# Attention in a two-layer model: TensorE's loop over pairs of heads rolled up, with one buffer each for the pair's operands

## The chip, the cores and the metric

One core of a Trainium2 chip (trn2) runs the whole kernel. The metric is the device time in microseconds (us) of one execution. Engines: PE is TensorE (PEld its weight loads), DVE is VectorE, ACT is ScalarE, POOL is GpSimd, SP is SyncE, which here only issues DMAs.

## The reference

The kernel computes two layers on 4 sequences of 1024 tokens with 256 channels, in float32. The change touches only the attention of the second layer:

```python
q = xn @ Wq;  k, v = split(xn @ Wkv)            # 16 heads of 64
q = apply_rope(pos, q);  k = apply_rope(pos, k);  q = q * SCALE
sim = einsum('bhid,bhjd->bhij', q, k)            # causal mask
attn = softmax(where(causal_mask, neg, sim))
out = einsum('bhij,bhjd->bhid', attn, v)         # then out @ Wo
```

After it comes a mixture of 8 experts with 2 chosen per token, and `x + s * silu(ffn)`. Whoever follows the change needs nothing more of them.

## The kernel before

The program runs in stages: the first layer (`normalize`, `first_layer`, `experts`), then `attention(nc, d, "at", 0, 3, True)` for the first three sequences (the first part below), then `moe`, the experts of the second layer, and then `attention(nc, d, "at2", 3, 1, False)` for the fourth sequence together with the closing sum of the whole output (the second part).

Attention goes over *pairs* of heads, 8 pairs for each sequence: 24 in the first part, 8 in the second. What each engine does in a pair is written as a list of events (`PE_ORDER`, `ACT_ORDER`, `DVE_ORDER`, lines 1192 to 1198). An event with a plus sign belongs to the pair after this one. TensorE's list is

```python
PE_ORDER = ("A0+ A1+ S4.1 S5.0 S5.1 S6.0 S6.1 S7.0 S7.1 A2+ T4.0 A4+ A5+ T5.0 T6.0 T6.1 A6+ T7.0 T7.1 S0.0+ S1.0+ S2.0+ S3.0+ V0 V1 S4.0+ "
            "W0 W1 W2 W3")
```

- **A** (lines 1593, 1599): projections of the next pair. A0 and A1 make queries and keys of the first half of the tokens, A4 and A5 of the second, A2 and A6 the values. ScalarE copies queries and keys to `raw` (line 1700) and the values to `v_top` (first half, keys 0 to 511) and `v` (line 1694).
- SP swaps the halves of each head by DMA (`swap`, line 1408), and GpSimd rotates: `rotate(of, half)`, lines 1720 to 1731, three operations for each half of the tokens, `raw * cos`, `swapped * sin` and their sum, into `qkT`.
- **S** (line 1608): scores from `qkT`. VectorE takes the running maximum (line 1901) and ScalarE the exponential (line 1675).
- **T** (line 1614): turns the late keys' probabilities, which ScalarE copies to `pT` (line 1686). VectorE transposes the others in blocks (line 1919).
- **V0** (line 1629): values of the first 512 keys in 32-row blocks, from `v_blocks`, which SP fills from `v_top` with 16 DMAs (`replicate`, line 1415). **V1** (line 1641): values of the other keys, from `v`. ScalarE copies the result (line 1706).
- **W** (line 1650): output projection with `wo`. VectorE adds it to the output (line 1938).

One event's results lie in PSUM banks used in turn; before an event PE waits until the bank's last reader is done (`free`, line 1546), and on what the event needs. Written out, one pair holds some 60 such waits on PE.

Two copies of `w` (projection weights), `wo`, `qkT` and `v` exist, used by even and odd pairs (`x = (u + ahead) % 2`). On ScalarE and SP the pairs are a hardware loop (`Fori`) whose body is two pairs (`run`, line 1356). On PE, VectorE and GpSimd Python writes all pairs out one after another; PE's lines are 1655 to 1658:

```python
                pairs = nb * PAIRS
                act_on("first", -1, -1, 1, -1)
                for it in range(pairs):
                    act_on("both" if it < pairs - 1 else "last", it, it % PAIRS, it % 2, it // PAIRS)
```

In SP's order `pair(it, ...)` (line 1418) issues the next output weights, the swaps of pair `it + 1`, the projection weights of pair `it + 3`, what the stage adds (`ready`) and the replication. Weights of pairs 0 and 1 and the first output weights are loaded during the first layer (`d.at_loads`, line 2190). In the first part GpSimd also sends token rows to experts with 8 indirect DMAs after each of 8 pairs' rotations (lines 1765 to 1785), and copies out a sequence (`end`). In the second part it closes the output between rotations: `begin` sums two gathered rows, ScalarE takes a tanh ahead of `T7.1` (line 1668), `plus` and `finish` do the rest.

Of the kernel before, what the change touches and what calls it, by code (L numbers as in the profile page):

```python
# [14 lines left out]
ds = bass.ds  # L15

P = 128
# [31 lines left out]
class Steps:  # L49
# [17 lines left out]
    def wait(self):  # L67
# [19 lines left out]
           "y_out w_in0 w_in1 wo_in0 wo_in1 a_ps qk_read v_read swap_in0 swap_in1 cosed sined rot_done blocks_in turned blocks_read s_ps exp_done inv_done s_seen s_read t_ps "  # L87
# [4 lines left out]
    "at2": ("steps less_max expd masks counted counts_read routed known h_in0 h_in1 h_ready0 h_ready1 y_out w_in0 w_in1 wo_in0 wo_in1 a_ps "  # L92
# [1182 lines left out]
def attention(nc, d, name, b0, nb, scatter):  # L1275

    with ExitStack() as ctx:
# [3 lines left out]
        qkT = [d.moe_ya[:, TB * C + u * 2 * T:TB * C + (u + 1) * 2 * T] for u in range(2)]  # L1281
        v_top, v = d.moe_w1[:, 0:HALF * P], [s.sb(f"v{u}", HALF * P) for u in range(2)]
# [45 lines left out]
        w_in, wo_in = s.sems("w_in"), s.sems("wo_in")  # L1328
# [50 lines left out]
        with nc.Block() as block:  # L1379
            @block.sync  # L1380
            def _(sp):
                if scatter:
                    sp.dma_start(number[:, :], d.number).then_inc(numbered, 16)
                for u in range(2):
                    sp.sem_inc(w_in[u], 16)
                    if u == 0:
                        sp.sem_inc(wo_in[u], 16)
                    sp.sem_inc(h_in[u], 16 * KC)
                    sp.sem_inc(h_ready[u], PAIRS)  # L1389
# [20 lines left out]
                def replicate(of):  # L1410

                    sp.wait_ge(blocks_read, of * HALF + ONE)
                    for b in range(QB):
                        for a in range(QB):
                            sp.dma_start(v_blocks[a * QR:(a + 1) * QR, b * HALF * P:(b + 1) * HALF * P],
                                         v_top[b * QR:(b + 1) * QR, :]).then_inc(blocks_in, 16)

                def pair(it, u, load_w, load_wo, half_free=lambda half: None, ready=lambda: None):

                    sp.wait_ge(w_ps, it * 4 + ONE)  # L1420
                    sp.dma_start(wo[1 - u][:, :], load_wo).then_inc(wo_in[1 - u], 16)
# [4 lines left out]
                    if load_w is not None:  # L1426
                        sp.dma_start(w[1 - u][:, :], load_w).then_inc(w_in[1 - u], 16)
# [3 lines left out]
                def next_w(i, u):  # L1431
                    return d.w["qkv"][ds(i * (2 * P) + (3 + u) * P, P), :], d.w["wo1"][:, ds(i * (2 * C) + (1 + u) * C, C)]
# [8 lines left out]
                sp.dma_start(w[0][:, :], d.w["qkv"][2 * P:3 * P, :]).then_inc(w_in[0], 16)  # L1441
                if nb > 1:
                    with sp.Fori(0, nb - 1) as b:
                        with sp.Fori(0, PAIRS // 2 - 2) as i:
                            for u in range(2):
                                pair(b * PAIRS + (i * 2 + u), u, *next_w(i, u))
                        pair(b * PAIRS + (PAIRS - 4), 0, d.w["qkv"][(PAIRS - 1) * P:PAIRS * P, :], wo_of(PAIRS - 3))
# [856 lines left out]
```

## Time and profile before

| | |
|---|---|
| three timed runs | 2503.62, 2504.72, 2507.83 us (median 2504.72) |
| the profiled execution | 2504.4 us, its span 2502.6 us |
| granted TensorE clock, mean | 0.962 of 2.4 GHz |
| busy: PE, PEld, DVE, ACT, POOL | 2293.1, 1644.2, 1391.0, 932.5, 899.5 us |
| attention, first part | from 801 to 1761 us |
| experts of the second layer | 1762 to 2161 us |
| attention, second part | 2168 us to the end |
| q8 instruction queue | 141 packets, 2.31 MB |
| q14 instruction queue | 74 packets, 0.61 MB |

Times in rows count from the start of the span. A timeline row is: start, length, engine, line, operation, names of output and inputs, shape, how many instructions were merged, and in brackets how long the engine had been idle and what ended that; "issue" means that the profile shows nothing it waited for.
### The profile page before, as it was taken

To read this page: it belongs to the slowest core of one execution; us is meant where nothing else is said; L and a number is where in the kernel's file an instruction comes from. 1 tells how busy PE (TensorE), PEld (TensorE's weight loads), DVE (VectorE), ACT (ScalarE), POOL (GpSimd) and SP (SyncE) were. 2 spreads that over 40 slices of the span, in tenths; PEclk is the share of its full clock that TensorE was granted. 3 is DMA by queue.
4 is the path that set the end of the run, shared out by engine and by line. 5 is a ranking of instruction groups with operands and counts; after the bars stand their busy time and mean duration, and the time that the engine had idled before them with its cause. 6 is when DMAs were issued, how large, how long until landed. Compare 5 with 4: busy or idle time off the path is not lost. (4 is left out here: it accounts for less than half of the span.)

```text
span 2502.6 us, 57008 instructions
## 1 busy us (share of the span) xinstructions
PE 2293.1 (92%) x20696; PEld 1644.2 (66%) x20697; DVE 1391.0 (56%) x3950; ACT 932.5 (37%) x2197; POOL 899.5 (36%) x659
## 2 busy tenths in 40 slices
PE   7999999999987688788899999998899999799995
PEld 5555556655565456556577666776899999666664
DVE  6675332222236856566677787776333333377685
ACT  3211111111125335344455655554222222264562
POOL 3002001554446445545534443442111111256761
PEclk9999999999998889999999999998999999999998
DMA  6013103975447233433332333333676776355441
GB/s 216 17 51 118 48 19 110 277 213 163 118 107 239 71 100 101 128 89 109 103 81 73 93 102 88 99 82 113 242 245 235 239 242 235 98 145 161 146 113 59
DMA packets 158631, 330.84 MB, mean 132 GB/s; under 512 B 25056, under 2 KB 95216, under 8 KB 148048
## 3 DMA queue, kind: packets, MB, share of 16 engines
q1 hardware_dynamic: 137472, 284.98, 36.7%
q0 software_dynamic: 20944, 42.94, 6.6%
q8 instruction: 141, 2.31, 0.4%
q14 instruction: 74, 0.61, 0.1%
HBM read 193.61 MB, written 67.12 MB: 104 GB/s over the span
## 5 line engine op out<-in xcount | busy, mean ns | idle before, releaser
L1675 ACT ACTIVATE at_p<-at_p,at_nmax 128x640 f32<-128x640 f32 (+7 forms) x512 | 393.2, 771 | 214.9 <-DVE at_nmax L1901 214.6
L1901 DVE CUSTOM_DVE_ANT_0 at_p<-at_ps,atk_mask 128x512 f32<-128x512 f32 (+3 forms) x512 | 281.1, 581 | 190.2 <-PE at_ps L1608 142.4
L1919 DVE STREAM_TRANSPOSE at_pB<-at_p 128x512 f32<-128x512 f32 (+3 forms) x512 | 279.4, 586 | 122.4 <-PE at_ps L1629 109.6
L1608 PE MATMUL at_ps<-kept_big 64*128 64x512 f32 (+3 forms) x1536 | 289.9, 510 | 36.9 <-POOL kept_big L1731 12.2
L1725 POOL TENSOR_TENSOR kept_big<-kept_xg,atk_cos 128x1024 f32<-128x1024 f32 x64 | 151.4, 2366 | 403.7 <-ACT kept_xg L1700 403.7
L1593 PE MATMUL at_ps<-atk_h,atk_w 128*128 128x512 f32 x512 | 241.0, 615 | 12.5 <-SPq L1389 12.5
L1629 PE MATMUL at_ps<-at_pB,at_v_blocks 32*64 32x256 f32 (+1 forms) x8192 | 209.2, 344 | 22.3 <-issue 15.9
L1608 PEld LDWEIGHTS at_ps<-kept_big 64*128 64x128 f32 x1536 | 133.5, 190 | 141.0 <-issue 45.1
L1629 PEld LDWEIGHTS at_ps<-at_pB,at_v_blocks 32*64 32x64 f32 x8192 | 183.6, 133 | 59.0 <-DVE at_nmax L1901 27.1
L1938 DVE SCALAR_TENSOR_TENSOR kept_big<-at_ps,at_inv,kept_big 128x256 f32<-128x256 f32 x512 | 203.7, 475 | 31.7 <-PE at_ps L1650 31.6
L1065 PE MATMUL ex_ps<-kept_big 128*128 128x512 f32 x480 | 210.2, 596 | 0.9 <-ACT kept_big L1122 0.9
L2020 POOL DMA_INDIRECT z_rows<-late_yo,late_to x71 | 68.8, 969 | 379.8 <-DVE late_yo L2103 379.8
L2042 PEld LDWEIGHTS moe_ps<-moe_xT,moe_w 128*128 128x128 f32 x1696 | 197.6, 192 | 3.9 <-ACT moe_xT L2075 1.2
L2042 PE MATMUL moe_ps<-moe_xT,moe_w 128*128 128x128 f32 x1696 | 198.0, 275 | 1.0 <-ACT moe_xT L2075 1.0
L1728 POOL TENSOR_TENSOR kept_xg<-kept_xg,atk_sin 128x1024 f32<-128x1024 f32 x60 | 142.1, 2368 | 132.3 <-DMA kept_xg<-kept_xg 132.3
L1593 PEld LDWEIGHTS at_ps<-atk_h,atk_w 128*128 128x128 f32 x512 | 95.1, 196 | 120.9 <-issue 90.8
L1065 PEld LDWEIGHTS ex_ps<-kept_big 128*128 128x128 f32 x480 | 91.7, 191 | 110.6 <-issue 109.9
L1700 ACT ACTIVATE kept_xg<-at_ps 128x512 f32<-128x512 f32 x128 | 76.6, 598 | 234.7 <-PE at_ps L1593 232.1
L1731 POOL TENSOR_TENSOR kept_big<-kept_big,kept_xg 128x1024 f32<-128x1024 f32 x64 | 151.4, 2365 | 21.3 <-DVE kept_xg L1923 12.4
L1650 PE MATMUL at_ps<-atk_wo,at_oT 64*128 64x256 f32 x1024 | 126.8, 400 | 32.4 <-ACT at_oT L1706 32.4
L1650 PEld LDWEIGHTS at_ps<-atk_wo,at_oT 64*128 64x128 f32 x1024 | 107.2, 202 | 61.9 <-ACT at_oT L1706 43.3
L1151 DVE TENSOR_TENSOR kept_big<-kept_big,ex_ps 128x512 f32<-128x512 f32 x64 | 44.0, 687 | 186.5 <-ACT kept_big L1127 175.5
(249 smaller groups left out, 3651.4 us busy)
## 6 DMA issues: line engine op xcount, KB each, us to landing
moe_w<-in_w_w SPq DMA_DIRECT2D x53, 1028.0 KB
kept_xg<-kept_xg SPq DMA_DIRECT2D x256, 128.0 KB, 2.3
at_v_blocks<-atk_first_w SPq DMA_DIRECT2D x512, 64.0 KB, 2.0
atk_first_w<-in_w_w SPq DMA_DIRECT2D x18, 1028.0 KB, 4.4
atk_w<-in_w_qkv SPq DMA_DIRECT2D x32, 384.0 KB, 3.2
slot_in<-kept_big SPq DMA_DIRECT2D x9, 1032.0 KB
kept_big<-in_w_eg SPq DMA_DIRECT2D x16, 512.0 KB
kept_big<-in_w_eu SPq DMA_DIRECT2D x16, 512.0 KB
```

Of the source, the lines that this page charges most:

```text
L1065: last = pe.matmul(bank, w[:, k * F0 + f * P:k * F0 + (f + 1) * P], xT[u][k][:, :], start=k == 0, stop=k == KC - 1)
L1593: last = pe.matmul(banks[0], w[x][:, k * QKV + m * P:k * QKV + (m + 1) * P], h[:, k * T + half * CH:k * T + (half + 1) * CH], start=k == 0 ...
L1608: pe.matmul(banks[e][:, 0:to - at], qkT[x][e * DH:(e + 1) * DH, n * P:(n + 1) * P], qkT[x][e * DH:(e + 1) * DH, T + at:T + to], start=True ...
L1629: last = pe.matmul(banks[a][e * DH:(e + 1) * DH, k * QR:TB * QR], v_blocks[rows, at:at + DH], keys[:, b], start=k == 0 and b == 0, stop=False)
L1650: last = pe.matmul(banks[e][:, t * C:(t + 1) * C], oT[rows, (2 * n + t) * P:(2 * n + t + 1) * P], wo[u][rows, :], start=True, stop=True)
L1675: act.activation(buf, buf, ACT.Exp, bias=nmax[:, unit:unit + 1], scale=-1.0, accum_out=rsum[:, unit:unit + 1]).then_inc(exp_done, 1)
L1725: pool.tensor_tensor(out=out, in0=plain, in1=cos_of, op=ALU.mult).then_inc(cosed, 1)
L1731: pool.tensor_tensor(out=out, in0=out, in1=other, op=ALU.add).then_inc(rot_done, 1)
L1901: ins = dve.tensor_tensor_reduce(out=p[unit % LAG][:, at:to], in0=ring[BANK_OF["S", (t, c), e]][:, 0:to - at], in1=mask[:, 0:CH] if to <= ...
L1919: dve.transpose(strided(pB[e][:, t * P:(t + 1) * P], TURN_STEP, keys), tiles(p[unit % LAG][:, 0:keys * P], keys)).then_inc(turned, 1)
L1938: dve.scalar_tensor_tensor(out=part_y, in0=bank[:, t * C:(t + 1) * C], scalar=inv[:, unit:unit + 1], in1=part_y, op0=ALU.mult, op1=ALU.add ...
L2042: last = pe.matmul(bank[:, m * P:(m + 1) * P], w1[q][:, at:at + P], xT[u][:, k * P:(k + 1) * P], start=k == 0, stop=k == KC - 1)
```

## The change

PE's pairs 1 to the last but one become one loop with a body of one pair. For that, what alternated by pair has one buffer:

- `qkT`: one. `rotate` waits until all scores of the pair before have been computed.
- `w`: one. It is loaded after the last projection of a pair, for the next pair. `wo`: one, loaded at the start of the pair that uses it.
- `v`: ScalarE writes the late values to `v_next`; SP copies `v_next` to `v` by one DMA after the replication, once V1 of the pair before is done. V1 waits for that DMA (`v_in`), and so does ScalarE before it writes `v_next` again.
- SP's loops go over single pairs. ScalarE keeps its loop of two, VectorE and GpSimd stay written out.

```diff
-        qkT = [d.moe_ya[:, TB * C + u * 2 * T:TB * C + (u + 1) * 2 * T] for u in range(2)]
-        v_top, v = d.moe_w1[:, 0:HALF * P], [s.sb(f"v{u}", HALF * P) for u in range(2)]
+        qkT = d.moe_ya[:, TB * C:TB * C + 2 * T]
+        v_top, v, v_next = d.moe_w1[:, 0:HALF * P], s.sb("v", HALF * P), s.sb("v_next", HALF * P)
...
                         for a in range(QB):
                             sp.dma_start(v_blocks[a * QR:(a + 1) * QR, b * HALF * P:(b + 1) * HALF * P],
                                          v_top[b * QR:(b + 1) * QR, :]).then_inc(blocks_in, 16)
+                    sp.wait_ge(o_ps, QB * of + ONE)
+                    sp.dma_start(v[:, :], v_next[:, :]).then_inc(v_in, 16)
...
-                def pair(it, u, load_w, load_wo, half_free=lambda half: None, ready=lambda: None):
+                def pair(it, load_w, load_wo, half_free=lambda half: None, ready=lambda: None):
 
                     sp.wait_ge(w_ps, it * 4 + ONE)
-                    sp.dma_start(wo[1 - u][:, :], load_wo).then_inc(wo_in[1 - u], 16)
+                    sp.dma_start(wo[:, :], load_wo).then_inc(wo_in, 16)
...
                     if load_w is not None:
-                        sp.dma_start(w[1 - u][:, :], load_w).then_inc(w_in[1 - u], 16)
+                        sp.dma_start(w[:, :], load_w).then_inc(w_in, 16)
...
                 replicate(0)
-                sp.dma_start(w[0][:, :], d.w["qkv"][2 * P:3 * P, :]).then_inc(w_in[0], 16)
+                sp.dma_start(w[:, :], w_of(1)).then_inc(w_in, 16)
...
-                        with sp.Fori(0, PAIRS // 2 - 2) as i:
-                            for u in range(2):
-                                pair(b * PAIRS + (i * 2 + u), u, *next_w(i, u))
...
+                        with sp.Fori(0, PAIRS - 2) as i:
+                            pair(b * PAIRS + i, *next_w(i))
...
                             if n == 0:
-                                pe.wait_ge(w_in[x], (it + u) * 8 + 16 + ONE)
+                                pe.wait_ge(w_in, of * 16 + ONE)
...
-                            pe.wait_ge(v_read, of * 2 + 2 + ONE)
+                            pe.wait_ge(v_in, of * 16 + 16 + ONE)
...
-                pairs = nb * PAIRS
-                act_on("first", -1, -1, 1, -1)
-                for it in range(pairs):
-                    act_on("both" if it < pairs - 1 else "last", it, it % PAIRS, it % 2, it // PAIRS)
+                act_on("first", -1)
+                act_on("both", 0)
+                with pe.Fori(1, nb * PAIRS - 1) as it:
+                    act_on("both", it)
+                act_on("last", nb * PAIRS - 1)
...
-                            act.activation(v[x][:, :] if half else v_top, ring[BANK_OF[kind, n, 0]], ACT.Copy).then_inc(v_read, 1)
+                            if half == 1:
+                                act.wait_ge(v_in, of * 16 + ONE)
+                            act.activation(v_next[:, :] if half else v_top, ring[BANK_OF[kind, n, 0]], ACT.Copy).then_inc(v_read, 1)
...
                     pool.wait_ge(qk_read, of * 4 + 2 * half + 2 + ONE)
-                    out = qkT[of % 2][:, :].rearrange("p (m t) -> p m t", m=2)[:, :, half * CH:(half + 1) * CH]
+                    pool.wait_ge(s_ps, of * PIECES_NO + ONE)
+                    out = qkT.rearrange("p (m t) -> p m t", m=2)[:, :, half * CH:(half + 1) * CH]
...
-            d.at_loads = [(d.at_w[u], d.w["qkv"][u * P:(u + 1) * P, :]) for u in range(2)]
-            d.at_loads += [(d.at_wo[0], d.w["wo1"][:, 0:C]), (d.at_cos, d.cos), (d.at_sin, d.sin), (d.at_mask, d.mask)]
+            d.at_loads = [(d.at_w, d.w["qkv"][0:P, :]), (d.at_cos, d.cos), (d.at_sin, d.sin), (d.at_mask, d.mask)]
```

## Rows read from the trace of the kernel before

**Rows 1.** Windows: stretch, its length, busy us (instructions) by engine, clock, DMA share, GB/s.
```profile
887.00:1194.00 307.00, 257.25 (x3282) 180.07 (x3279) 191.73 (x591) 139.48 (x336) 153.58 (x108) 0.91 0.37 106
...
1238.00:1723.00 485.00, 474.18 (x6558) 338.06 (x6554) 381.25 (x1178) 279.83 (x672) 202.33 (x86) 1.00 0.35 91
...
1800.00:2000.00 200.00, 200.00 (x1526) 192.57 (x1526) 69.80 (x252) 55.77 (x184) 35.71 (x37) 1.00 0.70 238
```

**Rows 2.** Timeline of PE, the shortest pair of the first part, and the next one's start.
```profile
1446.30 3.70 PE L1593 MATMUL at_ps<-atk_h,atk_w 128*128 128x512 f32 x8
1449.93 5.02 PE L1608 MATMUL at_ps<-kept_big 64*128 64x128 f32 x28
...
1464.27 2.43 PE L1608 MATMUL at_ps<-kept_big 64*128 64x128 f32 x16
1466.80 5.96 PE L1629 MATMUL at_ps<-at_pB,at_v_blocks 32*64 32x256 f32 x256
...
1476.24 3.62 PE L1650 MATMUL at_ps<-atk_wo,at_oT 64*128 64x256 f32 x32
1479.79 0.70 PE L1593 MATMUL at_ps<-atk_h,atk_w 128*128 128x512 f32 x1
```

**Rows 3.** Timeline of PE, first part: first and last row of fourteen pairs.
```profile
1238.43 3.70 PE L1593 MATMUL at_ps<-atk_h,atk_w 128*128 128x512 f32 x8
...
1719.75 3.62 PE L1650 MATMUL at_ps<-atk_wo,at_oT 64*128 64x256 f32 x32
```

**Rows 4.** Timeline of PE, second part: five pairs' first and last row, V1 in one.
```profile
2265.16 3.70 PE L1593 MATMUL at_ps<-atk_h,atk_w 128*128 128x512 f32 x8
...
2297.03 4.05 PE L1641 MATMUL at_ps<-at_pT,at_v 128*64 128x96 f32 x59 [3.12 <-issue]
...
2452.47 3.62 PE L1650 MATMUL at_ps<-atk_wo,at_oT 64*128 64x256 f32 x32
```

**Rows 5.** DMA queues: of 2293.5 to 2297.03, of 1273.25 to 1307.03, all of 476 to 640.
```profile
q8 instruction: 1, 0.02, 1.8%
...
q8 instruction: 4, 0.07, 0.8%
...
q1 hardware_dynamic: 9351, 24.50, 44.2%
q0 software_dynamic: 5856, 7.87, 23.4%
q14 instruction: 1, 0.01, 0.0%
```

**Rows 6.** Windows: one turn of the first layer's expert loop; one pair of attention.
```profile
476.26:562.32 86.06, 86.06 (x290) 51.95 (x289) 18.02 (x32) 13.47 (x24) 41.84 (x36) 1.00 0.77 234
1273.25:1307.03 33.78, 33.67 (x471) 24.31 (x469) 27.09 (x85) 19.96 (x48) 14.20 (x6) 1.00 0.31 78
```

**Rows 7.** Timelines of PE and POOL, a pair in which rows are sent.
```profile
972.72 5.40 PE L1650 MATMUL at_ps<-atk_wo,at_oT 64*128 64x256 f32 x32 [6.83 <-ACT at_oT L1706]
...
969.33 0.97 POOL L1784 DMA_INDIRECT slot_in<-kept_big,kept_tok_slot  x1 [0.30 <-issue]
```

**Rows 8.** Timelines of ACT, SP and PE, second part; last, weight loads from the DMA view.
```profile
2214.23 1.06 ACT L1668 ACTIVATE kept_big<-kept_big 128x1024 f32<-128x1024 f32 x1 [2.98 <-POOL kept_big L1743]
...
2224.95 0.38 ACT L1706 ACTIVATE at_oT<-at_ps 128x256 f32<-128x256 f32 x1 [0.23 <-PE at_ps L1641]
...
2283.32 1.08 ACT L1668 ACTIVATE kept_big<-kept_big 128x1024 f32<-128x1024 f32 x1
...
2193.52 0.58 SPq L1441 DMA_DIRECT2D atk_w<-in_w_qkv  x1
...
2191.28 5.39 PE L1593 MATMUL at_ps<-atk_h,atk_w 128*128 128x512 f32 x8
...
atk_w<-in_w_qkv SPq DMA_DIRECT2D x32, 384.0 KB, 3.2
```

**Rows 9.** Timeline of POOL, rotation of half 1 in the pair from 1410.69.
```profile
1434.01 2.35 POOL L1731 TENSOR_TENSOR kept_big<-kept_big,kept_xg 128x1024 f32<-128x1024 f32 x1
```

More of the change, by code:

```diff
@@ L1458, in next_h_ready @@
                             h_loaded(b + 1, 1)
[L1460 to L1461 removed]
+                        pair(b * PAIRS + (PAIRS - 2), w_of(0), wo_of(PAIRS - 2), next_h, ready=next_h_ready)
+                        pair(b * PAIRS + (PAIRS - 1), w_of(1), wo_of(PAIRS - 1))
                         store(b)
@@ L1487, in _ @@
                     sp.wait_ge(sent, 16 * TOP * NT)
-                    with sp.Fori(0, PAIRS // 2 - 2) as i:
-                        for u in range(2):
-                            pair(i * 2 + (it + u), u, *next_w(i, u))
-                            moe_weights(i * 2 + u)
-                    pair(it + PAIRS - 4, 0, d.w["qkv"][(PAIRS - 1) * P:PAIRS * P, :], wo_of(PAIRS - 3))
-                    moe_weights(PAIRS - 4)
-                    pair(it + PAIRS - 3, 1, d.w["qkv"][0:P, :], wo_of(PAIRS - 2))
-                    moe_weights(PAIRS - 3)
+                    with sp.Fori(0, PAIRS - 2) as i:
+                        pair(i + it, *next_w(i))
+                        moe_weights(i)
                     def last_h(half):
@@ L1532, in next_group @@
                             close_load(pr + 1)
-                        pair(pr, pr % 2, load_w, wo_of(pr + 1), ready=next_group)
+                        pair(pr, w_of(pr + 2) if pr + 2 < PAIRS else None, wo_of(pr), ready=next_group)
+                    sp.wait_ge(w_ps, (PAIRS - 1) * 4 + ONE)
+                    sp.dma_start(wo[:, :], wo_of(PAIRS - 1)).then_inc(wo_in, 16)
                     for n in range(TB // 2):
@@ L1564, in free, with act_on @@
                         pe.wait_ge(counts_read, 1 + ONE)
-                def act_on(part, it, pr, u, seq):
+                def act_on(part, it):
                     uses = ring_uses(part, scatter)
@@ L1569, in act_on @@
                         kind, n, ahead = ev
-                        of, x = it + ahead, (u + ahead) % 2
+                        of = it + ahead
                         if kind == "R" and not scatter:
@@ L1592, in act_on @@
                                 for k in range(KC):
-                                    last = pe.matmul(banks[0], w[x][:, k * QKV + m * P:k * QKV + (m + 1) * P],
+                                    last = pe.matmul(banks[0], w[:, k * QKV + m * P:k * QKV + (m + 1) * P],
                                                      h[:, k * T + half * CH:k * T + (half + 1) * CH], start=k == 0, stop=k == KC - 1)
```

46 lines of the change are left out of this document (20 added, 26 removed).

## The prediction

> **What bounds the kernel now.** I read the stage windows first, then TensorE's (PE's) timeline pair by pair, then the DMA queues in narrow windows. In the middle of the attention PE is busy 474 of 485 us; its work is back to back there, and VectorE is at 381 and ScalarE at 280 [rows 1]. A pair of heads takes 33.49 us where nothing goes wrong (1446.30 to 1479.79) [rows 2]. So PE is the bound, and only what stretches PE's pair counts.
>
> Four things stretch it. First, the fourteen pairs from 1238.43 to 1723.30 (the start of the last output projection, 1719.75, plus the 3.55 that the shortest pair has between 1476.24 and 1479.79) take 484.87 us, 34.63 each, not 33.49 [rows 2, 3]. Second, the five pairs from 2265.16 to 2456.02 (2452.47 plus 3.55) take 190.9 us, 38.2 each [rows 4]. The long ones stand still inside the value matmuls with nothing to wait for, 3.12 us in one of them, "issue" [rows 4]. During the 3.12 us one packet of the instruction queue q8 moves [rows 5]. One pair is 471 matmul and 469 weight-load records [rows 6] and draws 4 packets, 0.07 MB [rows 5]: some 235 to 256 instructions a packet. The top-row value matmuls are 256 short matmuls and 256 loads in 5.96 us [rows 2], two packets' worth at 12 ns an instruction, so a packet is used up in 3 us. PE has run out of program: before, its 32 pairs are written out one after another, and each instruction is fetched for one use. Third, the seven pairs in the stretch from 887 to 1194 take 43.9 each [rows 1]; six of them overlap the sending of rows to experts, so some 45.6 each if the seventh takes a clean pair's 33.5 ((307 - 33.5) / 6). There PE waits 6.83 us for the output that ScalarE copies, and goes on at 972.72, 2.4 us after GpSimd's last indirect DMA (969.33 + 0.97) [rows 7]. Fourth, the start of each attention part, where VectorE and the loads are late.
>
> **The change, part by part.**
>
> *PE's loop (removes).* From pair 1 on, 22 pairs of the first part and 6 of the second run in one loop body. Does the body stay on the chip? The expert loop of the first layer does: its turn is 290 + 289 records [rows 6], and between 476 and 640 us, nearly two turns, no q8 packet moves at all [rows 5]. That is 2.3 packets' worth held; the pair is 3.7 packets' worth, a little over 4 with register instructions. I take it as held. Then every turn but the first of each loop is free of fetch stalls. First part: 484.87 - 14 x 33.49 = 16.0 us. Second part: its clean pair is a little longer, since the gate's tanh, 1.08 us on ScalarE, sits ahead of a bank's reading [rows 8]; between 33.49 and 34.57 I take 33.9, some of the tanh being covered. The pair ahead of these five is the first turn and keeps its stall. The five after it give 190.9 - 5 x 33.9 = 21.4 us. Together **-37.4**. Bounds: 0 (not held) and, should the pairs with row sending also be waiting for program, five of the six (the sixth is the loop's first turn) x 11 us = 55 more.
>
> The Trainium skill (Runtime: NRT & Kernel Launch, section on instruction fetch mechanics) speaks against this change: it says that there are only two lines of 16 KiB, that fetching is purely sequential, and that a taken branch out of the window stalls on a fetch. By that rule every turn would stall; its price is the first rival's. The same section gives TensorE 128 KiB, 2048 instructions. The 579-record loop without one packet [rows 5, 6] contradicts two lines and agrees with the larger figure.
>
> *PE's loop (adds).* The thresholds of some 60 waits a pair are now worked out in registers, and there is a branch. No view shows these. Lower end: the expert tiles of the second layer are a PE loop with register waits, and PE is busy 200.00 of 200 us there [rows 1], so 0 where matmuls are queued. Upper end: five places in a pair where PE's queue can be empty (top values, bottom values, the score matmul after them, output projection, the next pair's head) x 0.23 us, the shortest reaction of ScalarE, which already runs a loop [rows 8]: 1.15. Only the bottom values start from a surely empty queue (short matmuls end as fast as they are issued); I take 0.2 x 22 undisturbed turns (16 in the first part, 6 in the second) = **+4.4**, bounds 0 and 25 (22 x 1.15). In the pairs with row sending the end is set by GpSimd, so nothing is added.
>
> *One buffer of rotated queries and keys.* GpSimd now starts rotation half 0 only when the last scores of the pair before have read the buffer: PE is through them 8.65 us into the pair (1449.93 + 5.02), and wants the new half at +17.97 (1464.27) [rows 2]. Three operations of 2.35 [rows 9] with 0.1 between make 7.3: ready at +16.0, 1.9 us early. Half 1 ended 25.7 us into a pair (1434.01 + 2.35, in the pair that begins at 1410.7) [rows 9], held by its inputs and not by GpSimd; 16.0 + 7.3 is earlier than that, so it ends as before, and it is needed just ahead of +29.9 (1476.24) [rows 2]. The row sending queued behind both rotations keeps its place, so the third stretch stays. In the second part the sum of the two gathered rows stands behind rotation half 0, so it ends at +18.4, and ScalarE, which reached its tanh at +18.2 (2283.32 - 2265.16) [rows 4, 8], waits 0.3 more; 7 pairs, **+2.3**. Where SP's loads make the swap late (the last pairs of the first part, which load expert weights) I add **+0.5**. Bounds 0 and, if the 1.9 us were not there, 2 us a pair, 58.
>
> *One buffer of projection weights.* In steady state the load is issued after the last read and is needed 20 us later; landing takes 3.2 [rows 8]: nothing. At the start of each part it costs: pair 1's weights were loaded ahead, now their load stands behind the 16 replication DMAs and the new copy. In the second part that is issued at 2193.52 + about 0.5 and lands at 2197.3, while PE wanted it at 2191.28 [rows 8]: 6 us late. Part of that was lost anyway, since the pair's tanh waited 2.98 us for GpSimd's sum and ended at 2215.3 [rows 8]. That chain now is: scores done at 2197.3 + 5.4 + 5.0 = 2207.7, rotation half 0 + 7.3, sum + 2.4, tanh + 1.1, so 2218.5, 3.2 later; with some for what follows **+3.6**, bounds 2 and 6. In the first part the same load comes 1.2 us after it is wanted; VectorE's routing bounds that pair: **+1**.
>
> *Output weights in one buffer.* Loaded at the pair's start, used 28 us later: nothing. *Later values through a transfer.* SP issues one DMA more, some 0.4 us, after the replication; it waits for the bottom values of the pair before, done long ago, and stands ahead of the next pair's swap, whose result now isn't wanted before +11. ScalarE's and PE's waits on it have most of a pair. Nothing; if SP were late by 2 us the swap would be the next wait.
>
> **Sum.** -37.4 + 4.4 + 2.3 + 0.5 + 3.6 + 1 = -25.6. Against the profiled execution's own 2504.4 us (span 2502.6, 1.8 around it; the median of the three timed runs is 2504.7, the same): **2479 us**.
>
> **Rivals.**
> 1. *The body isn't held* (slower). 26 backward jumps meet an empty store. For it: 3.7 packets are more than the 2.3 seen held. Against it: the same view [rows 5]. The price is one stall a turn as in [rows 4], 3.1 us less what PE has queued; at 2 us, 52, and the -37.4 isn't had: 2504.4 + 12 + 52 = 2568. It decides as soon as a packet is drawn every turn. By the Trainium skill's two-line rule this is the outcome. Chance 0.09.
> 2. *Register waits are dear.* The gain is there, but 1 to 1.15 us a turn goes to thresholds behind late releases: -37 + 25 + 7 = -5, 2499. For it: a wait in a straight program is one immediate; against it: the expert tiles' row. Chance 0.14.
> 3. *The row-sending pairs were fetch-bound as well.* 2479 - 55 = 2424. For it: "issue" and late matmuls appear in them. Against it: their end follows GpSimd's last DMA by the same 2.4 us. Chance 0.09.
> 4. *Rotation comes late* at the one buffer: over 1.9 us lost somewhere in GpSimd's 7.3. At 1 us a pair over 22 turns, 2479 + 22 = 2501: no change. Chance 0.06.
> 5. *Nothing moves*: fetch stalls come from traffic and stay. Chance 0.04, 2512.
>
> **How the numbers follow.** The forecast, 0.58, has 2465 to 2490 as its own range (the register term 0 to 12, starts 2 to 8, stalls 35 to 42). For 8 in 10 the range takes in rivals 2 and 4 and part of 3: 2450 to 2502. About 0.2% (5 us) is what a measurement of this kernel can tell from no change. Faster by more than that: forecast, rival 3, and most of 2 and 4, 0.79. Slower: rivals 1 and 5 and a tail of 2, 0.13. Same: 0.08.
>
> **What would show it.** q8 draws no packet in the middle of either attention part, where it drew 4 a pair; "issue" ahead of the value matmuls is gone; pairs are all about 33.7 in the first part and 34.4 in the second. Rotation half 0's first operation starts 8.7 us into a pair and its last ends by +16.1. The row-sending pairs still take some 45 us. PE waits some 6 us for projection weights at the second part's start. Packets in every turn, or a wait at each pair's head, prove rival 1; constant pairs of 34.7 or more, rival 2; short row-sending pairs, rival 3; PE waiting for GpSimd before the new pair's scores, rival 4.

## The result, and the profile after

| | kernel before | kernel changed |
|---|---|---|
| timed runs, median (4 each) | 2506.27 us | 2477.03 us |
| range | 2503.62 to 2508.22 | 2475.20 to 2478.55 |
| ratio, 95% interval | | 0.9884, 0.9867 to 0.9901 |
| span of the profiled execution | 2502.6 us | 2475.4 us |
| q8 instruction packets | 141 | 44 |

The change makes the kernel 29 us faster. The forecast was 2479.

The queues' part of the page of the changed kernel, and the DMA view of two stretches: the first part from the start of pair 10 (1272.46) to 1700, and the second part's loop (2258.2 to 2428). Columns: packets, MB, share of 16 engines.

```profile
q8 instruction: 44, 0.72, 0.1%
q14 instruction: 73, 0.60, 0.1%
...
q1 hardware_dynamic: 23207, 43.19, 37.4%
q14 instruction: 18, 0.15, 0.1%
...
q1 hardware_dynamic: 13301, 25.97, 52.7%
q14 instruction: 10, 0.08, 0.2%
```

There is no line for q8 in either stretch: TensorE's program isn't fetched once in twelve whole pairs and most of a thirteenth, nor in the second part's five, where it drew 4 packets a pair before [rows 5].

Stage windows of the changed kernel: pairs 1 to 7 (rows are sent), the fourteen undisturbed pairs 9 to 22, and pairs 2 to 6 of the second part. Columns as in [rows 1].

```profile
889.53:1195.94 306.41, 252.14 (x3278) 180.39 (x3276) 190.97 (x589) 140.25 (x336) 153.56 (x108) 0.89 0.38 110
1239.16:1707.18 468.02, 466.25 (x6554) 335.60 (x6552) 379.58 (x1177) 280.76 (x672) 202.28 (x86) 1.00 0.37 100
2258.16:2428.18 170.02, 167.60 (x2342) 118.05 (x2340) 135.17 (x420) 104.97 (x245) 120.61 (x54) 1.00 0.53 153
```

The fourteen pairs took 484.87 us [rows 3] and take 468.02, which is 33.43 each; the five took 190.86 [rows 4] and take 170.02, 34.00 each. Pairs 1 to 7 are as long as they were (307 in [rows 1]). One pair of the first part on PE, the same as in [rows 2], with the start of the next:

```profile
1439.31 3.70 PE L1588 MATMUL at_ps<-atk_h,atk_w 128*128 128x512 f32 x8
1442.94 5.00 PE L1603 MATMUL at_ps<-kept_big 64*128 64x128 f32 x28
...
1457.26 2.43 PE L1603 MATMUL at_ps<-kept_big 64*128 64x128 f32 x16
1459.68 5.90 PE L1624 MATMUL at_ps<-at_pB,at_v_blocks 32*64 32x256 f32 x256
1465.50 2.66 PE L1636 MATMUL at_ps<-at_pT,at_v 128*64 128x128 f32 x64
1468.09 1.13 PE L1603 MATMUL at_ps<-kept_big 64*128 64x512 f32 x4
1469.06 3.62 PE L1645 MATMUL at_ps<-atk_wo,at_oT 64*128 64x256 f32 x32
1472.61 1.12 PE L1588 MATMUL at_ps<-atk_h,atk_w 128*128 128x512 f32 x2
```

33.30 us from head to head, and 11 of the 14 pairs are this length to 0.01 us (the last one by the start of its output projection). No wait is left between rows. The branch lies between the last two and shows no gap: the output projection is still running while TensorE's sequencer takes it (0.208 us in the trace of its instructions).

The one place that got longer is the start of the second part. PE there, and the DMA view of 2208.5 to 2211.8, inside the gap of 2.75 us:

```profile
2181.28 5.48 PE L1588 MATMUL at_ps<-atk_h,atk_w 128*128 128x512 f32 x8 [6.14 <-issue]
...
2204.22 4.76 PE L1624 MATMUL at_ps<-at_pB,at_v_blocks 32*64 32x256 f32 x182
2211.74 2.64 PE L1624 MATMUL at_ps<-at_pB,at_v_blocks 32*64 32x192 f32 x74 [2.75 <-issue]
...
q1 hardware_dynamic: 233, 0.82, 61.9%
q8 instruction: 1, 0.02, 1.8%
```

PE is idle for 6.14 us ahead of the new pair's projections (their weights are still on the way), and then stands 2.75 us inside the value matmuls, while one packet of its program comes in among 0.82 MB of other data. This pair runs from code that isn't in the loop.

Where the 27.2 us between the two spans are, stretch by stretch, by the start of each pair on PE:

| stretch | before | after | difference |
|---|---|---|---|
| up to pair 0 | 800.90 | 800.17 | -0.73 |
| pair 0 of the first part | 86.36 | 89.36 | +3.00 |
| pairs 1 to 8 (rows sent) | 351.16 | 349.63 | -1.53 |
| pairs 9 to 22, with 1.4 us of waiting after them | 486.30 | 469.44 | -16.86 |
| last pair and experts | 443.85 | 443.78 | -0.07 |
| pair 0 of the second part | 62.01 | 69.64 | +7.63 |
| pair 1 (first turn of the loop) | 34.58 | 36.13 | +1.55 |
| pairs 2 to 6, with 1.4 us after them | 192.28 | 171.44 | -20.84 |
| last pair | 31.03 | 31.71 | +0.68 |

### The profile page after: what moved, and what is told of

Read it like the earlier page. It is cut to its first block and busy times, and to the rows that moved or that the text cites. A ratio compares the mean times of both kernels' runs of the same rounds, so it can differ in the third digit from the quotient of the medians.

```text
span 2475.4 us, 58172 instructions
## 1 busy us (share of the span) xinstructions
PE 2283.6 (92%) x20696; PEld 1647.3 (67%) x20697; DVE 1390.1 (56%) x3950; ACT 936.5 (38%) x2197; POOL 900.0 (36%) x659
## 5 line engine op out<-in xcount | busy, mean ns | idle before, releaser
L1603 PE MATMUL at_ps<-kept_big 64*128 64x512 f32 (+3 forms) x1536 | 287.8, 509 | 28.1 <-POOL kept_big L1730 10.5
L1624 PEld LDWEIGHTS at_ps<-at_pB,at_v_blocks 32*64 32x64 f32 x8192 | 183.3, 134 | 45.9 <-issue 38.7
L1624 PE MATMUL at_ps<-at_pB,at_v_blocks 32*64 32x256 f32 (+1 forms) x8192 | 203.2, 344 | 10.6 <-issue 7.0
```

Of the source, the lines that this page charges most:

```text
L1603: pe.matmul(banks[e][:, 0:to - at], qkT[e * DH:(e + 1) * DH, n * P:(n + 1) * P], qkT[e * DH:(e + 1) * DH, T + at:T + to], start=True, stop ...
L1624: last = pe.matmul(banks[a][e * DH:(e + 1) * DH, k * QR:TB * QR], v_blocks[rows, at:at + DH], keys[:, b], start=k == 0 and b == 0, stop=False)
```

## The experiments

The theory: what the change brings is program fetching that the loop saves, and nothing else of it brings anything. The rivals: the single buffers or the shorter loops on SP have a part in it; or the loop would do as well with any body. Every ratio below is to the kernel before, run in the same series, that is on the same chip and at the same time. There were five series: the result; the written-out run with the bodies of two and three pairs and the two buffers; the weights first, the rows four a pair and the first two filled bodies; the body of 1498 and the two runs with later loads; the run with early loads.

### TensorE written out again

```diff
-                with pe.Fori(1, nb * PAIRS - 1) as it:
+                for it in range(1, nb * PAIRS - 1):
                     act_on("both", it)
```

> The changed kernel with TensorE's pairs written out again, everything else (one buffer each, the values through a transfer) as it is. Theory (the gain is program fetching that the loop saves): the stalls come back, 4 packets a pair on q8 and some 140 in all, the fourteen undisturbed pairs at about 34.6 and not 33.4, second part's pairs about 38 and not 34; and the single buffers keep what they cost at the two starts (3.0 and 7.6 us by the pairs' table): 2477 + 17 + 20 = 2514 us, so 8 us slower than before. Rival A (the single buffers or SP's shorter loops made the pairs regular, for instance by moving transfers): stays below 2490. Rival B (single buffers cost nothing at the starts, those 7.6 us are an accident of code placement): 2504 to 2507.

Measured: ratio to the kernel before 1.0034 (1.0012 to 1.0056), some 8 us slower, and on its page:

```profile
q8 instruction: 141, 2.31, 0.4%
```

By the pairs' starts the fourteen undisturbed pairs take 484.4 us again, 34.60 each; the shortest is 33.52. The second part's pairs 2 to 5 take 41.25, 37.47, 38.70 and 35.16 us (40.37, 39.67, 36.33 and 34.72 in the kernel before), and pairs 2 to 6 together 192.4. Against the changed kernel, which differs from this one by the loop alone, the loop saves 16.3 us in the first of these stretches and 22.4 in the second. The second part's pair 0 takes 68.00 us (62.01 before), the first part's 88.85 (86.36). The theory's 2514 was 8 us above the kernel before, which is what came out. Rivals A and B fall: the single buffers gain nothing and cost 8.5 us at the two starts (6.0 + 2.5).

### Two and three pairs in the body

```diff
-                with pe.Fori(1, nb * PAIRS - 1) as it:
-                    act_on("both", it)
+                with pe.Fori(0, (nb * PAIRS - 2) // 2) as i:
+                    for u in range(2):
+                        act_on("both", i * 2 + (1 + u))
```

> The changed kernel with a loop body of two pairs, some 1996 instructions and not 998. Theory (TensorE holds at least some 2000 instructions of its program): no packets of q8 in the middle of the parts, 2477 +- 4 us. Rival (it holds the four to five packets that one pair needs, but not eight): 8 packets a turn, stalls as in the kernel before, 2505 to 2515; if each backward jump also waits for its packet, 14 x 3 us more, up to 2555.

Measured: ratio 1.0104 (1.0064 to 1.0144), 26 us slower than the kernel before, with 170 packets. PE at the end of a turn, and the DMA view of the two pairs from 1357.7 to 1428.7:

```profile
1387.97 3.62 PE L1645 MATMUL at_ps<-atk_wo,at_oT 64*128 64x256 f32 x32
1394.17 2.41 PE L1588 MATMUL at_ps<-atk_h,atk_w 128*128 128x512 f32 x5 [2.58 <-DVE kept_big L1938]
...
q8 instruction: 10, 0.16, 0.9%
```

The theory's size was wrong: 1993 instruction records a turn aren't held. The 2.58 us ahead of the next pair's first matmul are put down to VectorE, but in the record of the branch itself TensorE's sequencer sits 3.4 to 4.1 us, against 0.208 in the changed kernel. Over all runs here whose body isn't held a backward jump takes 3.3 to 4.2 us. Of this 2.2 to 2.8 show on PE as idle time in the first part's undisturbed pairs. After four of these seven jumps the clock is lower as well: the next pair's first matmuls take up to 5.39 us in place of 3.70, at a mean granted clock of 0.68 of 2.4 GHz in that pair (1248.41 to 1253.80). The stalls inside the pairs are back as well: with 36.2 us an undisturbed pair it is worse than written out.

For three pairs:

> The changed kernel with a loop body of three pairs, some 2994 instructions. Theory (a store of about eight packets, 2048 instructions, that drops the oldest): every turn draws its 12 packets again, the stalls of the written out program come back, 2477 + 37 = 2514, and the 7 + 2 turns' backward jumps cost 0 to 3 us each, so 2510 to 2540 us. Rival (a part of the body stays, or the store is larger): below 2495 us and clearly fewer than 4 packets a pair.

Measured: ratio 1.0056 (1.0039 to 1.0074), 155 packets, 13 in a turn of 2988 records, jumps of 3.4 to 3.9 us. The theory had 12 packets and 2510 to 2540 us; the median is 2526. Its interval overlaps that of the written-out run, so it isn't shown to be slower than that one. Against the body of two it jumps less often (7 + 2 turns against 11 + 3), but that is only part of the difference: the fourteen undisturbed pairs take 484 us here and 506 there, with four jumps in them against six. The rest lies in shorter stalls and a clock that dropped once and not four times, and what makes that difference stays open.

### Two buffers, and only the loop changed

```diff
-                for it in range(pairs):
-                    act_on("both" if it < pairs - 1 else "last", it, it % PAIRS, it % 2, it // PAIRS)
+                act_on("both", 0, 0, 0, 0)
+                with pe.Fori(0, (pairs - 2) // 2) as i:
+                    for u in (1, 0):
+                        act_on("both", i * 2 + (2 - u), None, u, None)
+                act_on("last", pairs - 1, PAIRS - 1, 1, nb - 1)
```

> The kernel before with its two buffers each, and only TensorE's loop changed: pairs 1 to the last but one in a hardware loop whose body is two pairs. Theory (the loop is the whole gain, the single buffers only cost, and 2000 instructions are held): no packets in the middle, undisturbed pairs of 33.3 us, and neither start costs more: 2506 - 17 - 20 = 2469 us, 8 below the changed kernel. Rival A (a body of two pairs isn't held): 2505 to 2550. Rival B (the single buffers bring part of the gain): 2477 or above with no packet drawn.

Measured: ratio 1.0082 (1.0055 to 1.011), 170 packets, jumps of 3.3 to 4.2 us: rival A. With buffers for even and odd pairs a body must hold two pairs, and two pairs aren't held. This is what the single buffers are for: they gain nothing themselves, but without them the loop loses.

### How much is held

The changed kernel with short matmuls repeated, to fill the body:

```diff
+                            if n == 0:
+                                for _ in range(250):
+                                    pe.matmul(banks[0][:, 0:32], qkT[0:DH, 0:P], qkT[0:DH, T:T + 32], start=True, stop=True)
                             for e in range(2):
```

> The changed kernel with 250 short matmuls repeated ahead of the first scores of each pair (they write 32 columns that the next matmul overwrites), which makes the loop body some 1498 instructions, 5.9 packets, and adds some 6 us of work a pair. It is to find how much program TensorE holds: 998 instructions are, 1996 are not. If up to 7 packets are held (eight less the one fetched ahead): no packet of q8 in the middle, the jump takes 0.2 us. If at most five: 6 packets a turn and a jump of 3.3 to 4 us, as in the body of two pairs.

> The same with 375 repeated matmuls: 1748 instructions, 6.8 packets. If seven packets are held wherever the body begins: no packet in the middle and a jump of 0.2 us. If the packet fetched ahead and the unaligned ends of the body (it touches eight packets) push the first one out: 7 packets a turn and jumps of 3.3 to 4 us.

These two missed their sizes: such a matmul is four records, so the bodies (250 and 375 of them) were 1998 and 2498. Both are not held (10 and 12 packets a turn, jumps of 3.3 to 4.1 us), which repeats what the body of two pairs said. Their times (5817 and 7517 us) only tell what the repeated matmuls cost. With 125 of them the body is 1498:

> The changed kernel with 125 short matmuls repeated ahead of the first scores of each pair (they write 32 columns that the next matmul overwrites). The two runs before showed that one such matmul is four records and not two, so that their bodies were 1998 and 2498 instructions, both not held. This one is some 1498, 5.9 packets. If up to seven packets are held (eight less one fetched ahead): no packet of q8 in the middle of the parts, a backward jump of 0.2 us. If four or five packets are all (1024 to 1280 instructions): 6 packets a turn and a jump of 3.3 to 4 us. Its time says nothing: a repeated matmul takes some 0.42 us, about 52 us a pair, 32 pairs, some 4150 us in all.

The DMA view of this kernel from 1146.5 to 1660, six turns, and PE over the repeated matmuls:

```profile
q1 hardware_dynamic: 10785, 18.95, 13.8%
q0 software_dynamic: 3008, 9.48, 5.6%
q14 instruction: 9, 0.07, 0.0%
...
1080.40 51.09 PE L1604 MATMUL at_ps<-kept_big 64*128 64x32 f32 x249
```

No line for q8, and jumps of 0.208 us: 1498 records are held. So the limit lies between 1498 and 1993, and the body of one pair (998) is well inside. The Trainium skill (Runtime: NRT & Kernel Launch, section on instruction fetch mechanics) gives TensorE a store of 2048 instructions. A turn of 1993 to 1998 records (7.8 packets) would fit into that and drew 10; whether a part of the store is taken by what is fetched past the loop's end wasn't tested. The page's two lines, with a stall on a jump out of them, are what these runs exclude for TensorE: the body of 1498 records is 5.9 packets.

### The starts

At the start, the load of pair 1's projection weights ahead of the replication:

```diff
-                replicate(0)
                 sp.dma_start(w[:, :], w_of(1)).then_inc(w_in, 16)
+                replicate(0)
```

> The changed kernel, with the load of pair 1's projection weights ahead of the 16 replication DMAs and the values' transfer instead of behind them. Theory (at the second part's start PE waits 6.1 us for these weights, and rotation and the later steps follow): the load is issued some 11 us earlier, the idle 6.1 us ahead of A0+ shrinks to 0 to 1, but the pair's tanh then waits for GpSimd's sum again, so that the pair gets 3 to 4 us shorter (69.6 to 66), or 6 to 7 if the fetch stall of 3.1 us in its value matmuls goes with it; the first part's pair 0 gains up to 3: 2477 - 3.5 - 2 = 2471 us. Rival (something else ends last in that pair, such as the loads of the closing sum or VectorE): PE's idle moves from the weights to another wait and the time is 2476 to 2478.

Measured: ratio 0.9838 (0.9819 to 0.9858), against the changed kernel's 0.9884 (0.9867 to 0.9901). In the second part's first pair:

```profile
2175.65 5.92 PE L1588 MATMUL at_ps<-atk_h,atk_w 128*128 128x512 f32 x8
...
2198.95 1.13 PE L1603 MATMUL at_ps<-kept_big 64*128 64x512 f32 x4 [1.55 <-ACT at_pT L1682]
2200.01 4.76 PE L1624 MATMUL at_ps<-at_pB,at_v_blocks 32*64 32x256 f32 x182
2208.31 3.06 PE L1624 MATMUL at_ps<-at_pB,at_v_blocks 32*64 32x192 f32 x74 [3.54 <-issue]
```

The 6.14 us of idle are gone, which shows that they were the weights; 1.55 us of waiting for ScalarE are new, and the stall in the value matmuls has grown to 3.54. The pair takes 66.52 us in place of 69.64, the first part's pair 0 87.95 in place of 89.36. The profiled execution is only 1.3 us shorter than the changed kernel's, at 2475.9 us the longest of four whose others are 2464.0 to 2466.3; the 11 us between the medians are more than its pairs show, and where the rest comes from stays open.

Then the stall. By the theory the packet queues behind 2 MB that SP loads for the closing sum of the next group. With the weights first as above, these loads moved behind the replication, in that pair alone:

```diff
-                    ready()
+                    if not late:
+                        ready()
                     replicate(it + 1)
+                    if late:
+                        ready()
...
-                        pair(pr, w_of(pr + 2) if pr + 2 < PAIRS else None, wo_of(pr), ready=next_group)
+                        pair(pr, w_of(pr + 2) if pr + 2 < PAIRS else None, wo_of(pr), ready=next_group, late=pr == 0)
```

> The changed kernel with two moves in SP's order: pair 1's projection weights ahead of the replication (as in the run above), and in the first pair of the second part the loads of the closing sum (2 MB) behind the replication instead of ahead of it. Theory (the 3 to 4 us that TensorE stands in that pair's value matmuls is a packet of its program queued behind those loads): the stall falls to 0.5 to 1.5 us and the pair from 66.5 to 63.5; 2 to 3 us faster than with the first move alone: 2463 us. Rival A (the stall is the price of a packet used up faster than it is fetched, whatever else moves): same as with the first move alone, 2466. Rival B (the sum of the next pair now comes late and holds the tanh): the next pair gets longer by 1 to 4 us, 2467 or more.

Measured: ratio 0.9848 (0.9834 to 0.9861). It can't be set beside the 0.9838 of the weights alone, since the kernel before took 2427 us in this series (see the pairs that send rows, below). The pairs can: the first took 61.25 us, without the stall (from the first of the top value matmuls to the first of the bottom ones, V0 to V1, 6.10 us in place of 11.29), and the next took 41.52 in place of 36.96, so that the two together gain 0.7 us over the weights alone. In that next pair GpSimd waits for a swap, and PE for GpSimd:

```profile
2146.23 2.37 POOL L1730 TENSOR_TENSOR kept_xg<-kept_xg,atk_sin 128x1024 f32<-128x1024 f32 x1 [5.15 <-DMA kept_xg<-kept_xg]
...
2151.22 1.83 PE L1606 MATMUL at_ps<-kept_big 64*128 64x128 f32 x12 [3.31 <-POOL kept_big L1733]
```

Rival B's effect, by another way than it said: not the sum but the swap was late, since its DMAs stood behind the same loads.

The trace also shows where the packet was. PE runs the same program in the changed kernel, with the weights first and here. The packet that is fetched during V0 starts to move 5.07 and 5.95 us after V0's first matmul in the first two and 1.86 us after it here, and takes 0.9 to 1.2 us in all three: it was late to start, not slow.

The same move in all pairs of the kernel before, where TensorE is written out:

> The kernel before, TensorE written out, with one move: in all pairs of the second part the loads of the closing sum behind the replication. Theory (the stalls of 3.1 to 4.1 us in the second part's value matmuls are packets that queue behind these loads, while without them they are 0.5 to 1.7 us as in the first part): the long stalls fall to under 2 us, the second part's pairs from 38.2 to some 36: 2506 - 8 = 2498 us. Rival A (traffic doesn't matter): stalls as before, 2506. Rival B (loads issued some 12 us later hold the sum, and the tanh with it, or the swaps behind them come late): pairs of 38 and more with other waits, 2506 to 2520.

Measured: ratio 1.015 (1.0135 to 1.0166), 36 us slower than the kernel before, more than any of the three had. One of its pairs:

```profile
2215.17 2.34 POOL L1731 TENSOR_TENSOR kept_xg<-kept_xg,atk_sin 128x1024 f32<-128x1024 f32 x1 [13.94 <-DMA kept_xg<-kept_xg]
...
2220.13 2.93 PE L1611 MATMUL at_ps<-kept_big 64*128 64x128 f32 x12 [7.66 <-POOL kept_big L1734]
...
2225.07 5.91 PE L1632 MATMUL at_ps<-at_pB,at_v_blocks 32*64 32x256 f32 x256
...
2232.23 2.44 PE L1644 MATMUL at_ps<-at_pT,at_v 128*64 128x96 f32 x59 [0.79 <-issue]
```

Both sides are in these rows. The long stalls in the value matmuls of the second part, three of 3.3 to 4.1 us in the kernel before, measured from the start of one short matmul to the start of the next, are down to 1.04 at most. And GpSimd stands 13.9 us until the swap is there, which makes pairs of 41 to 45 us. This run alone doesn't show that the stalls were packets behind the loads, since PE also waits 2.5 to 7.7 us for GpSimd ahead of the value matmuls, and its program can come in meanwhile; in pair 0, above and below, the stall goes with the loads without a new wait of that size. So the second part's stalls, twice as long as the first part's 1.7 us, were fetching and traffic together.

Last of these, again with the weights first, the same loads earlier, between the swaps of the two halves, where nothing behind them is urgent (their buffers are free from the start):

```diff
-                            close_load(pr + 1)
-
-                        pair(pr, w_of(pr + 2) if pr + 2 < PAIRS else None, wo_of(pr), ready=next_group)
+                            if pr > 0:
+                                close_load(pr + 1)
+
+                        def early_load(half):
+                            if pr == 0 and half == 0:
+                                close_load(1)
+
+                        pair(pr, w_of(pr + 2) if pr + 2 < PAIRS else None, wo_of(pr), early_load, ready=next_group)
```

> The changed kernel with two moves in SP's order: pair 1's projection weights ahead of the replication, and the loads for the second group of the closing sum (2 MB, their buffers are free from the start) earlier in the first pair of the second part, between the swaps of half 0 and half 1, instead of behind both. In the run with these loads moved later the packet stall in that pair was gone (V0 to V1 6.1 and not 11.3 us) but the next pair got 4.6 us longer, since its swaps stood behind the loads. Theory (no transfer of size is under way when TensorE's packet is wanted, and nothing behind the loads is urgent): the pair some 62 us and the next 36 to 37, 4 to 5 us less than with the weights alone, a ratio to the kernel before of 0.982 (2461 us where before has 2506). Rival (the swaps of half 1 come late behind the loads and hold the rotation that the upper scores need): the pair 65 to 67, ratio 0.984. Whether the row-sending pairs take 45 or 33 us here isn't known: they took 45 in three series of runs and 33 in the last one.

Measured: ratio 0.9843 (0.9816 to 0.987). PE in the same pair:

```profile
2118.16 1.13 PE L1608 MATMUL at_ps<-kept_big 64*128 64x512 f32 x4 [2.31 <-ACT at_pT L1687]
2119.22 5.91 PE L1629 MATMUL at_ps<-at_pB,at_v_blocks 32*64 32x256 f32 x256
2125.06 2.66 PE L1641 MATMUL at_ps<-at_pT,at_v 128*64 128x128 f32 x64
```

No stall: the pair takes 61.26 us and the next 37.72, together 98.98 against 105.77 in the changed kernel, 103.48 with the weights alone, 102.77 with the loads later and 96.59 in the kernel before. The ratio of 0.982 that was expected is inside the interval but isn't shown; nor can it be set beside the 0.9884, since this series ran where the row-sending pairs are short (below) and the kernel before took 2424 us. Shown faster than both kernels is the one with the weights first alone, whose interval lies below the changed kernel's in series where the kernel before took 2506 us. That the two with moved loads are better still is told by their pairs alone (4.5 us less than with the weights first for this one, 0.7 for the one before), across series, and not by a time.

### The pairs that send rows

```diff
-                        j = of - 1
-                        if 0 <= j < TOP * B:
+                        j, part = (of - 1) // 2, (of - 1) % 2
+                        if 0 <= j < TOP * B and part == 0:
...
-                            for n in range(TB):
+                        if 0 <= j < TOP * B:
+                            at = j // B * NT + j % B * TB
+                            for n in range(part * (TB // 2), (part + 1) * (TB // 2)):
```

> The changed kernel, with GpSimd's row sending spread: 4 indirect DMAs behind the rotations in each of 16 pairs instead of 8 in each of 8. This tests what holds the row-sending pairs, which the change left at 45 us. Theory (an output projection can't start until 2.4 us after the last indirect DMA, whatever TensorE's program does): four of them end some 31 us into a pair, PE starts the output projection at 33.5 and not at 29.8, so sixteen pairs of 37 us in place of six of 45.4, one of 43.2 and the tail of pair 0: about -81 + 60 = 20 us less, 2457. Rival A (the jam has a fixed length however many are sent): sixteen long pairs of 45, 2477 + 90 = 2567 us. Rival B (the delay only comes with more than four in a row): 2477 - 80 = 2400 us.

Measured: ratio 0.9901 (0.9871 to 0.9932), 2481.9 us: no gain. GpSimd's last send of a pair and PE's output projection in it; then the output projection of the changed kernel in the same pair:

```profile
1036.61 0.97 POOL L1785 DMA_INDIRECT slot_in<-kept_big,kept_tok_slot  x1 [0.30 <-issue]
...
1039.63 5.40 PE L1645 MATMUL at_ps<-atk_wo,at_oT 64*128 64x256 f32 x32 [3.73 <-ACT at_oT L1704]
```

```profile
1020.08 5.84 PE L1645 MATMUL at_ps<-atk_wo,at_oT 64*128 64x256 f32 x32 [9.33 <-issue]
```

All three theories missed. The start of the output projection follows the last send as said (1037.58 + 2.05), but the pairs are 39.7 us, not 37: twelve pairs with four sends take 6.4 us more than 33.30, 1.6 a send, and six pairs with eight take 12.2 more, 1.5 a send. It grows with the number of sends. Not all of it is waiting: once PE has stood idle, the output projection itself takes 5.40 and 5.84 us in these rows in place of 3.62, at a mean granted clock of 0.68 and 0.63 of 2.4 GHz.

This price isn't one of the kernel alone. In the last two series the same sends took the same time on GpSimd and held nobody; in a pair of the run with early loads:

```profile
1010.67 3.62 PE L1650 MATMUL at_ps<-atk_wo,at_oT 64*128 64x256 f32 x32
...
1017.12 0.97 POOL L1788 DMA_INDIRECT slot_in<-kept_big,kept_tok_slot  x1 [0.31 <-issue]
```

The output projection starts 29.75 us into the pair while six of the eight sends are still to come. In the loop all row-sending pairs but the first and the last are 33.3 to 35.6 us there, and the kernel before took 2424 to 2427 us in place of 2506 to 2511. Nothing in the kernel before differs, and it isn't the chip either: it took 2507 us in the third series and 2427 in the fourth, minutes apart on the chip with the same number. What makes the difference wasn't found.

## Why the prediction was right

The time (2479 against 2477.03), the mechanism and the view that would show it (q8 without a packet in the middle of both parts, the "issue" ahead of the value matmuls gone) came out. Step by step:

- **Fetch stalls gone, -37.4.** The two stretches of undisturbed pairs are 37.7 us shorter (16.86 + 20.84), and that has in it what registers and rotation cost there; against the written-out run, which has the single buffers too, it is 38.7 (16.3 + 22.4). The written-out run gives the stalls back and the loops of two pairs don't save them, so this term is shown to be fetching. My argument that the body is held took the expert loop (579 records, 2.3 packets) to a body of 3.7 packets without a row in between; it held, but with less room than "held" suggested: the next natural body, two pairs, would have failed.
- **Register waits, +4.4, bounds 0 and 25.** Measured nothing, or less than nothing: the shortest pair went from 33.49 [rows 2] to 33.30, and 33.52 when written out again; the value matmuls begin 20.37 us into it, not 20.50. This is the term that was mis-sized, and its lower bound was wrong: I had no reason to exclude a gain. Of the 0.19 us, 0.13 lies ahead of the value matmuls, where the written-out pairs have 0.11 us of "issue" and the loop's have none. That isn't fetching: the body of three pairs isn't held and starts them at 20.37 too. What it is stays open.
- **Rotation at one buffer.** In time, as said: the first operation starts 8.8 us into a pair (1414.82 in the pair from 1406.01) and the last ends at 16.0; scores start at 17.95 as before. In the second part the value matmuls begin at 21.07, not 20.93: 0.14 us a pair, 1 us in seven, where I had 2.3 (and seven times my 0.3 is 2.1).
- **Projection weights at the start of the second part, +3.6.** PE was idle 6.14 us where I had 6, and the value matmuls began 3.45 us later into the pair (51.84 against 48.39) where I had 3.2. But the pair got 7.63 longer: the other 4.2 us are a fetch stall and the matmuls behind it (V0 to V1 10.09 in place of 6.51, and 0.6 in V1), which run at a mean granted clock of 0.70 after it. I had costed the pairs outside of the loops at no change, and their packets come when they come: where the pair was shifted against the closing sum's loads, the stall grew. The runs that moved those loads show that cause by taking it away.
- **Start of the first part, +1.** Measured +3.0. The value matmuls begin 3.0 us later into the pair (63.37, 60.33 before) and run into the row sending, which holds them: 17.1 us in place of 10.8 from V0 to V1, given back in V1.
- **Row sending.** These pairs stayed at 45 us, so rival 3 didn't happen. (Its price was 11 us a pair, where my own 45.6 less 33.5 gives 12.) Where the sends don't hold PE it would have been partly right: in the series of the two runs with later loads, pairs 1 to 6 take 208.6 us written out and 202.9 in the loop.
- **First turns.** The loop's first turn in the second part took 1.55 us more than the written-out pair, and PE waits 1.56 us for VectorE ahead of its output projection there. I had it as equal.

For the two stretches of undisturbed pairs I had, all terms together, 31.5 us less (37.4 less 3.8 of the registers, 1.6 of the rotation and 0.5 of the swap) and got 37.7; for all the rest I had 5.9 more and got 10.5. The two errors, 6.2 and 4.6 us, nearly cancelled in the sum, so the closeness of forecast and result says less than it seems to.

## What to carry to other kernels

An engine that issues hundreds of short instructions in a row can use up its program faster than it comes; the sign is idle time put down to "issue" in the middle of a run of the same instruction, with a packet of the instruction queue inside it. A hardware loop cures it only if its whole body stays on the chip (1498 records did here, 1993 didn't); if it doesn't, each turn also pays 2 to 3 us for the jump, and the loop of two pairs was worse than the written-out program. To make the body small enough, buffers that alternate can be worth giving up, and what that costs lies at the start, where loads that used to be ahead now queue behind others: order SP's first DMAs anew.

## What the runs showed of the hardware

- A backward jump of TensorE takes 0.208 us when its target is held and 3.3 to 4.2 us when it isn't. Turns that aren't held draw one to two packets more than they have instructions for (10 packets for 1993 records, 13 for 2988).
- A packet of the program takes its place among the data: stalls (start to start of two short matmuls) that are at most 1.7 us in the first part were 3.3 to 4.1 in the second, behind 2 MB of loads. With those loads moved out of the way in pair 0, the packet started 1.86 us into the value matmuls in place of 5.95, and the stall was gone.
- A stall costs more than its length. After 3.12 us without an instruction the granted clock was 0.57 in the next 4 us (2297.03 to 2301.02), and the bottom value matmuls took 4.05 us where the changed kernel has 2.66; after a jump that wasn't held it was 0.68, and after the waits in the row-sending pairs 0.63 and 0.68.
- GpSimd's indirect DMAs made the pair they were sent in 1.5 to 1.6 us longer each in the first three series (the 1.8 to 2.2 us that the output projection loses to the lower clock included), and next to nothing in the last two. The kernel before took 2506 to 2511 us in the ones and 2424 to 2427 in the others.
- A 32-column float32 matmul onto the same columns again and again takes 0.205 us a record (51.09 us for 249), as two records and two weight loads; the mean granted clock was 0.52 of 2.4 GHz while they ran.
